# Linear attention and self-attention of a perceiver kernel: scores of a whole token tile issued over four row groups, outcomes of two or four units together, one sum moved to GpSimd

## The reference, cut to what matters

```python
# linear attention: 16 heads of 32; rho is a decay per token and head
S = r * S + (1.0 - r) * jnp.einsum('bhv,bhk->bhvk', v_t, k_t)
y_t = jnp.einsum('bhv,bhvk->bhk', q_t, S)
# self-attention: 16 heads of 64, rotary q and k, causal
scores = jnp.einsum('bhqd,bhkd->bhqk', q, k) * scale
attn = jax.nn.softmax(jnp.where(causal, scores, -jnp.inf), axis=-1)
ctx = jnp.einsum('bhqk,bhkd->bhqd', attn, v)
```

## Time and profile before

| | us |
|---|---|
| median of 3 runs | 2023.27 (2022.45 to 2024.18) |
| the profiled execution's own time | 2018.79 |
| its span | 2017.1 |
| PE busy | 1900.9 (94%), 10722 matmul instructions |
| PEld busy | 1293.5 (64%) |
| DVE busy | 691.0 (34%) |
| ACT busy | 561.0 (28%) |
| POOL busy | 201.3 (10%) |
| mean granted TensorE clock | 0.976 |

### The profile page before, as it was taken

The page is one execution under the profiler, slowest core; times in us unless marked ns, Lnnn a source line. Parts: engine busy times, 40 slices in busy tenths (PEclk is TensorE's granted clock), DMA queues, the critical chain, the costliest instruction groups (busy, mean ns, idle before and its releaser), DMA issues.

```text
span 2017.1 us, 26698 instructions
## 1 busy us (share of the span) xinstructions
PE 1900.9 (94%) x10722; PEld 1293.5 (64%) x10722; DVE 691.0 (34%) x1706; ACT 561.0 (28%) x1263; POOL 201.3 (10%) x293
## 2 busy tenths in 40 slices
PE   5999999999999999998999978999898999999995
PEld 3677777777548447555777755777545544777773
DVE  4234344343335654421000145555425322111111
ACT  2333333332123224212222235444425200111110
POOL 0000000000010232322111031111001110000001
PEclk9999999999999998999999998999899999999998
DMA  5011111101320010027999730102212300877762
GB/s 194 22 42 43 37 69 43 42 22 64 125 104 1 21 42 30 36 83 259 352 354 352 277 119 32 48 32 90 105 42 84 149 22 16 318 289 285 284 252 80
DMA packets 43802, 245.19 MB, mean 122 GB/s; under 512 B 5929, under 2 KB 6433, under 8 KB 20880
## 3 DMA queue, kind: packets, MB, share of 16 engines
q1 hardware_dynamic: 30752, 213.22, 28.7%
q0 software_dynamic: 6000, 17.58, 2.7%
q10 hardware_dynamic: 6912, 12.52, 1.6%
HBM read 227.73 MB, written 15.57 MB: 121 GB/s over the span
## 4 chain that ended last, share of the span: by engine, by line
PE 86%; DVE 5%; issue 5%; DMA 2%; POOL 1%; ACT 1%; POOLq 0%; SPq 0%; DVEq 0%; ACTq 0%
PE bank L224 25%; PE bank L548 25%; PE bank L1606 10%; PE bank L230 8%; PE bank L690 3%; PE bank L718 2%; PE bank L2483 2%; PE bank L637 2%; PE bank L644 2%; PE bank L1186 2%; PE bank L1590 1%; PE bank L983 1%; PE bank L997 1%; PE bank L1211 1%; PE bank L975 1%
## 5 line engine op out<-in xcount | busy, mean ns | idle before, releaser
L548 PE MATMUL bank<-split 128*128 128x512 f32 x2208 | 549.1, 401 | 24.9 <-DVE split L521 12.3
L548 PEld LDWEIGHTS bank<-split 128*128 128x128 f32 x2208 | 407.3, 190 | 155.6 <-issue 31.6
L224 PEld LDWEIGHTS bank<-arena,weights 128*128 128x128 f32 x1984 | 229.7, 187 | 36.1 <-issue 33.7
L224 PE MATMUL bank<-xnT,weights 128*128 128x512 f32 (+1 forms) x592 | 246.7, 577 | 4.7 <-DVE xnT L880 3.1
L224 PE MATMUL bank<-arena,weights 128*128 128x128 f32 (+1 forms) x1984 | 245.1, 282 | 2.8 <-DVE arena L1597 1.8
L224 PEld LDWEIGHTS bank<-xnT,weights 128*128 128x128 f32 x592 | 113.2, 193 | 132.1 <-issue 124.8
L1606 PE MATMUL bank<-weights,arena 128*128 128x512 f32 (+1 forms) x368 | 166.6, 596 | 0.0
L230 PE MATMUL bank<-weights,arena 128*128 128x512 f32 x288 | 131.9, 611 | 8.3 <-ACT arena L2366 6.0
L1606 PEld LDWEIGHTS bank<-weights,arena 128*128 128x128 f32 (+1 forms) x368 | 65.9, 190 | 72.6 <-issue 72.6
L2593 DVE SCALAR_TENSOR_TENSOR arena<-bank,cols,arena 128x128 f32<-128x128 f32 x96 | 28.8, 345 | 230.7 <-PE bank L224 227.9
L230 PEld LDWEIGHTS bank<-weights,arena 128*128 128x128 f32 x288 | 54.8, 196 | 73.3 <-issue 62.9
(11 more groups left out here) (284 smaller groups left out, 2014.5 us busy)
## 6 DMA issues: line engine op xcount, KB each, us to landing
weights<-in_L_ffn_re_w SPq DMA_DIRECT2D x62, 1024.0 KB, 8.2
weights<-in_L_w SPq DMA_DIRECT2D x20, 1408.0 KB, 12.0
arena<-in_ctxT SPq DMA_DIRECT2D x24, 1024.0 KB, 5.0
arena<-in_L_w SPq DMA_DIRECT2D x12, 1408.0 KB, 7.6
weights<-in_L_w_full SPq DMA_DIRECT2D x10, 1280.0 KB, 9.5
expert_out<-arena ACTq DMA_DIRECT2D x47, 256.0 KB, 8.3
weights<-in_L_ffn_sw SPq DMA_DIRECT2D x9, 1024.0 KB, 5.0
arena<-in_L_w_full SPq DMA_DIRECT2D x6, 1280.0 KB, 9.8
```

The costliest lines, as they stand in the source:

```text
L224: s = pe.matmul(out, w[:, k, j0:j0 + m], rhs(k), start=(k == 0), stop=(k == KT - 1))
L548: s = pe.matmul(bank[:, :], still, moving, start=(n == 0), stop=(n == len(order) - 1))
```

## The change

**Linear stage.** TensorE issues the scores of all four units of a token tile together, 16 matmuls of the source into four banks, the strip (row group) changing from one to the next, and the outcomes of the four units of a tile together as 16 matmuls of 32 columns, each into the partitions of its own strip of one bank. They are issued when the spread of the next tile's first unit has been issued. The spreads get two banks, `decay` eight buffers. GpSimd forms mask - L_j for each unit (`less`, four buffers), and VectorE adds it to the spread in one instruction of 512 columns. ScalarE copies the outcome of a whole tile at once (four copies of 128 partitions for sixteen of 32).

**Self-attention stage.** The scores of a tile are likewise issued together over four row groups into four banks, which all have to be read by the mask instructions before those of the next tile may start. Transposes have two banks, outcomes one, values one. The outcomes of two units are issued together as 8 matmuls of 64 columns in two column groups, and one VectorE instruction of 128 partitions adds the bias for both. `self_probT` has four buffers for two. The value groups 3 to 7 move to units 1, 3, 5, 7 and 9.

```diff
     def linear_tensor(pe):
+        def scores(i):
+            if i:
+                pe.wait_ge(lin_decayed.sem, lin_decayed.at(4 * i))
+            for hm in range(KT):
+                for j in range(4):
+                    r = 32 * j
+                    s = pe.matmul(banks[j][:, hm * P:(hm + 1) * P], lin_vT[r:r + 32, hm, i * P:(i + 1) * P],
                                   lin_qT[r:r + 32, hm, i * P:(i + 1) * P], start=True, stop=True)
+            s.then_inc(lin_scored.sem, 1)
+
+        def outcome(i):
+            pe.wait_ge(lin_decayed.sem, lin_decayed.at(4 * i + 4))
+            if i >= 2:
+                pe.wait_ge(lin_out, i - 1)
+            for hm in range(KT):
+                for j in range(4):
+                    r, h = 32 * j, 4 * hm + j
+                    s = pe.matmul(banks[6 + i % 2][r:r + 32, hm * P:(hm + 1) * P], k_tok[:, i, 32 * h:32 * h + 32],
+                                  decay[(4 * i + j) % 8][:, hm, :], start=True, stop=True)
+            s.then_inc(lin_valued.sem, 1)
+
+        for t in range(LN):
+            i, j = LIN_UNITS[t]
+            if t >= 2:
+                pe.wait_ge(lin_logged, t - 1)
+            for hm in range(KT):
+                c = i * HEADS + 4 * hm + j
+                s = pe.matmul(banks[4 + t % 2][:, hm * P:(hm + 1) * P], lg["L"][:, c:c + 1].to_broadcast([P, P]),
+                              ident[:, :], start=True, stop=True)
+            s.then_inc(lin_spread.sem, 1)
+            if j == 0:
+                scores(i)
+                if i:
+                    outcome(i - 1)
+        outcome(NT - 1)
...
     def linear_vector(dve):
-                for hm in range(KT):
-                    c = i * HEADS + 4 * hm + j
-                    s = dve.scalar_tensor_tensor(out=decay[t % 4][:, hm, :], in0=banks[3 + t % 3][:, hm * P:(hm + 1) * P],
-                                                 scalar=lg["minus_L"][:, c:c + 1], in1=mask_ji[:, :], op0=ALU.add,
-                                                 op1=ALU.add)
-                s.then_inc(lin_logged, 1)
+                dve.wait_ge(lin_pool.sem, lin_pool.at(2 + t + 1))
+                if t >= 8:
+                    dve.wait_ge(lin_valued.sem, lin_valued.at((t - 8) // 4 + 1))
+                dve.tensor_tensor(decay[t % 8], blocks(banks[4 + t % 2][:, :], KT), less[t % 4],
+                                  ALU.add).then_inc(lin_logged, 1)
...
     def linear_gpsimd(pool):
+        for t in range(LN):
+            i, j = LIN_UNITS[t]
+            if t >= 4:
+                pool.wait_ge(lin_logged, t - 3)
+            pool.tensor_tensor(less[t % 4], over_middle(mask_ji[:, :], KT), over_last(blocks(lg["minus_L"], NT)[:, i, j::4], P),
+                               ALU.add).then_inc(lin_pool.sem, 1)
...
-    VALUES_FIRST, VALUES_THEN, VALUES_AT = (0, 1), (2,), {0: 3, 1: 4, 4: 5, 8: 6, 12: 7}
+    VALUES_FIRST, VALUES_THEN, VALUES_AT = (0, 1), (2,), {1: 3, 3: 4, 5: 5, 7: 6, 9: 7}
...
     def selfattn_tensor(pe):
+        def scores(i):
+            if i == 0:
+                pe.wait_ge(rope_v, 8 * 2)
+            else:
+                pe.wait_ge(self_masked.sem, self_masked.at(4 * i))
+            for hm in range(KT):
+                for half, (qq, kk) in enumerate(((q1, k1), (q2, k2))):
+                    for j in range(4):
+                        r = 32 * j
+                        s = pe.matmul(banks[j][:, hm * P:(hm + 1) * P], qq[r:r + 32, hm, i * P:(i + 1) * P],
+                                      kk[r:r + 32, hm, i * P:(i + 1) * P], start=(half == 0), stop=(half == 1))
+            s.then_inc(self_scored.sem, 1)
+
+        def outcome(pair):
+            if pair >= 1:
+                pe.wait_ge(self_out.sem, self_out.at(pair))
+            pe.wait_ge(self_prob.sem, self_prob.at(2 * pair + 2))
+            for hm in range(KT):
+                for half in range(2):
+                    h, m = 4 * hm + 2 * (pair % 2) + half, 2 * pair + half
+                    s = pe.matmul(banks[6][64 * half:64 * half + 64, hm * P:(hm + 1) * P], v_tok[:, i, 64 * h:64 * h + 64],
+                                  self_probT[m % 4][:, hm, :], start=True, stop=True)
+            s.then_inc(self_valued.sem, 1)
+
         for t in range(LN + 3):
+            if t < LN and t % 4 == 0:
+                scores(t // 4)
             if t in VALUES_AT:
                 values(VALUES_AT[t])
             if 2 <= t < LN + 2:
+                turn(t - 2)
+            if t >= 4 and t % 2 == 0:
+                outcome(t // 2 - 2)
```

More of the change, by code:

```diff
@@ L927, in build_program @@
     decay = [L(KT, P) for _ in range(4)]
+    L(3 * SEQ)
+    decay += [L(KT, P) for _ in range(4)]
+    less = [L(KT, P) for _ in range(4)]
     G = NT * HEADS
@@ L1001, in linear_tensor @@
+        outcome(NT - 1)
+        pe.wait_ge(lin_out, NT)
         output_tensor(pe, 1, yT, ["lin_o"], xn)
@@ L1079, in linear_scalar, with outcome @@
             act.copy(lin_vT[:, m, :], banks[m][:, :]).then_inc(lin_a.sem, 1)
-        for t in range(LN + 2):
-            if t < LN:
-                act.wait_ge(lin_logged, t + 1)
-                act.activation(decay[t % 4], decay[t % 4], ACT.Exp).then_inc(lin_exped.sem, 1)
-            if t >= 2:
-                n = t - 2
-                i, j = LIN_UNITS[n]
-                r = 32 * j
-                act.wait_ge(lin_valued.sem, lin_valued.at(n + 1))
-                act.copy(yT[r:r + 32, :, i * P:(i + 1) * P], blocks(banks[6 + n % 2][r:r + 32, :], KT)).then_inc(lin_out, 1)
+        def outcome(i):
+            act.wait_ge(lin_valued.sem, lin_valued.at(i + 1))
+            act.copy(yT[:, :, i * P:(i + 1) * P], blocks(banks[6 + i % 2][:, :], KT)).then_inc(lin_out, 1)
+        for t in range(LN):
+            act.wait_ge(lin_logged, t + 1)
+            act.activation(decay[t % 8], decay[t % 8], ACT.Exp).then_inc(lin_exped.sem, 1)
+            if t % 4 == 1 and t > 4:
+                outcome(t // 4 - 1)
+        outcome(NT - 1)
         def roots(i):
@@ L1117, in build_program @@
     soft = [L(KT, P) for _ in range(4)]
-    self_probT = [L(KT, P) for _ in range(2)]
+    self_probT = [L(KT, P) for _ in range(4)]
     pos, turns = L(SEQ), L(SEQ)
@@ new lines, in turn @@
+        def turn(m):
+            if m >= 2:
+                pe.wait_ge(self_prob.sem, self_prob.at(m - 1))
+            pe.wait_ge(self_normed, m + 1)
+            for hm in range(KT):
+                s = pe.transpose(banks[4 + m % 2][:, hm * P:(hm + 1) * P], soft[m % 4][:, hm, :], ident[:, :])
+            s.then_inc(self_turned.sem, 1)
+        def outcome(pair):
+            i = pair // 2
+            if pair % 2 == 0:
+                pe.wait_ge(self_a.sem, self_a.at(4 * KT + 2 * (i + 1)))
+            if pair >= 1:
+                pe.wait_ge(self_out.sem, self_out.at(pair))
+            pe.wait_ge(self_prob.sem, self_prob.at(2 * pair + 2))
+            for hm in range(KT):
+                for half in range(2):
[3 more added lines that the diff above has]
+            s.then_inc(self_valued.sem, 1)
```

128 lines of the change are left out of this document (31 added, 97 removed).

## The result

The changed kernel takes 1990.5 us (median of 4 runs, 1988.3 to 1996.9) where the kernel before, measured beside it, takes 2022.9 (4 runs, 2019.1 to 2024.2). The ratio is 0.9847, with a 95% interval of 0.9829 to 0.9864: faster by 32 us. The forecast was 1998.3: the direction held, the gain was larger than forecast, and the time lies inside the range. Most of the mechanism held as well; the price of the clock in the second stage did not.

What follows compares the result with a forecast made beforehand. TensorE was taken to end both stages, 135.5 us together. Winning 3 us in the linear and 22 in the self-attention stage, 25 off the median 2023.3, gave 1998.3 us; 80% range 1986 to 2012.

Steps and rivals of the forecast that it cites:

- Overlap of row and column groups: Scores and outcomes, both stages: four row or column groups of matmuls run at once, 0.111 us per four.
- no overlap: Rival, chance 0.05: row groups serial, scores cost 3.6 us per linear and 7.1 per self tile; 2030 us.
- The linear cycle: Linear stage, per unit: the VectorE and ScalarE chain of sum, exp and product sets the cycle, 2.16 us.
- the rival of exclusion: Rival, chance 0.05: GpSimd and VectorE exclude each other in the linear stage, 1.04 us more per unit; 2011 us.
- The tile boundary: Linear stage: VectorE waits for the spread behind scores and outcome on TensorE, 0.95 us at each of three boundaries.
- The clock in the linear stage: Half clock at one boundary, the last outcome and the projection takes 7 of 9.7 us won; 3 stay.
- The self-attention stage at full clock: Self-attention stage: TensorE-paced part 32.4 us, then ScalarE exps, last scores and tail; sum 55 us, 30 won.
- The clock in the self-attention stage: Half clock near the start, late in the self-attention stage and in its projection takes 8 us; 22 stay.
- Clock holds: Rival, chance 0.14: full clock in both stages, 40 us won less 4 or so for the tails; 1987 us.
- Half clock throughout: Rival, chance 0.04: half clock through both stages, self-attention 87 us, linear 50 to 52; 2032 us.
- only two row groups: Rival, chance 0.12: only two row groups overlap, score time doubles, 3.6 us more in linear, 7 in self-attention; 2008 us.
- Nothing behind takes it back: Rest of the program: expert stretches are TensorE-bound and weights are requested by use, so later stages lose nothing.

Runs made afterwards that it cites:

- strip-by-strip order: Changed kernel with all score matmuls of one row group issued before those of the next, in both stages: 2035.9 us, ratio 1.0067 to the kernel before.
- the kernel with fillers throughout: Changed kernel plus unread 512-column matmuls before the linear stage's last outcome and, from the third unit, each spread except the second strip's: 1986.5 us, ratio 0.9819.
- the two kernels with fillers: Changed kernel plus unread matmuls ahead of the linear stage's last outcome only (1992.7 us), or also ahead of most spreads (1986.5 us).
- the runs with this stage alone: Changed kernel with the self-attention stage put back as in the kernel before, only the linear stage changed: 2019.0 us, ratio 0.9984.
- all of them together: Changed kernel plus filler matmuls (at spreads, first and last strip only), old tile's outcome behind the new tile's second spread, value groups at 1, 5, 9, 13, 15: 1977.9 us.
- the outcome later: Changed kernel with the old tile's linear outcome issued behind the new tile's second spread instead of ahead of it: 1990.6 us, ratio 0.9830.
- the values later: Changed kernel with value groups 3 to 7 at units 1, 5, 9, 13, 15 in place of 1, 3, 5, 7, 9: 1989.6 us, ratio 0.9827.

## Why the prediction was right or wrong

**Overlap of row and column groups: right.** This carried the forecast. The forecast was 0.9 us for 32 linear score matmuls and 1.8 for 64 self ones; measured, with a change of shape in each, 1.11 and 2.00. Two row groups, or none, would have given twice or more. The estimate that was drawn from the Trainium skill (TensorE: Matmul & The Clock Gate, "Measured speedup vs the span model", 3.07 times for four row tiles) would have made the linear group 32 x 0.111 / 3.07 + 0.20 = 1.36; the trace has 1.11, so here it was close to four times. The strip-by-strip order comes near the rival "no overlap", which was to decide below some 1.3 times: 2.75 us per group, which is 1.4 times (0.111 for 0.080), and a time above that of before. The forecast had priced that rival at 2030. The order came to 2035.9, but not by the rival's sum: of its 45 us over the changed kernel some 20 are the order at full clock, the rest goes with half clock.

**The linear cycle: right in kind, 0.17 us too long.** Sum starts at 607.05 and 609.03, in the lines

```profile
607.05 0.68 DVE L1061 TENSOR_TENSOR arena<-bank,arena 128x512 f32<-128x512 f32 x1
608.42 0.69 DVE L1054 TENSOR_TENSOR arena<-bank,arena 128x512 f32<-128x512 f32 x1 [0.70 <-ACT arena L1091]
609.03 0.68 DVE L1061 TENSOR_TENSOR arena<-bank,arena 128x512 f32<-128x512 f32 x1
```

give 1.98 for the 2.16 of the sum. The sum follows 0.61 us after the start of the product ahead of it (609.03 - 608.42), before that product's 0.69 has ended, and the forecast had laid them end to end. `less` takes 1049 ns for the 1.04 forecast, VectorE's sum beside it 684 ns for 0.69, and GpSimd waits for VectorE, not the other way: the rival of exclusion is out.

**The tile boundary: mis-sized.** The forecast gave 0.95 us to each of three, at full clock. With the clock held, in the kernel with fillers throughout, sums on either side of a boundary stand 614.81 - 611.37 = 3.44 apart, 1.45 more than a cycle (L1066 is the sum there, L1002 the spread):

```profile
611.37 0.68 DVE L1066 TENSOR_TENSOR arena<-bank,arena 128x512 f32<-128x512 f32 x1
...
614.81 0.69 DVE L1066 TENSOR_TENSOR arena<-bank,arena 128x512 f32<-128x512 f32 x1 [1.31 <-PE bank L1002]
```

The path was right: scores, outcome and the new tile's second spread follow each other on TensorE. Its length was not. VectorE has the spread 3.36 us after the end of the old tile's last product (611.45), where the forecast had 3.12: the spread's group takes 1.16 us until its result is there, not 0.89. And VectorE wants it 1.9 us after that product, not 2.16, as its cycle is shorter. In the changed kernel the three are 5.01, 4.96 and 6.14 apart, 10.1 us in excess of three cycles. The longer cycle (15 x 0.17 = 2.6 us) and the shorter boundary (3 x 0.5 = 1.5 us) of the forecast largely cancelled: its full-clock stage was 40.3, and the stage with a clock of 1.00, fillers included, takes 40.2. That they meet so closely is luck.

**The clock in the linear stage: right as a total.** 7 of 9.7 us were to go to half clock, 4.3 at the end and 2.7 at one boundary. Measured by the two kernels with fillers, 45.5 - 40.2 = 5.2 in the stage and 11.55 - 8.77 = 2.8 in the projection: 8.0. There were four falls (611.8, 622.0, 632.3 and 645.9) and not two, so boundaries paid more and the end less than forecast; the second profile of the changed kernel has three. What stays is 4.6 - 2.8 = 1.8 us for the 3 of the forecast, and the runs with this stage alone agree (ratio 0.9984).

**The self-attention stage at full clock: right as a sum.** 55 us were forecast. Taking from 58.0 what half clock cost, 1.5 at the first scores (3.47 for 2.00) and 1.4 at 789.34 (0.5 for the transposes, 0.9 for the outcome), leaves 55.1. Its two parts were right as well. The first, with three scores, five value groups, seven transposes and three outcomes, ends where the last value group does, at 771.78: 34.0 us after the start, less 1.5 of half clock, is 32.5 for the 32.4 forecast; in the second profile, without half clock, it takes 32.6. What follows takes 24.0, less 1.4, which is 22.6 for 22.5.

**The clock in the self-attention stage: the step that failed.** 8 us of the 30 were to go; 2.9 went. At the start it cost 1.5 us for the 1.7 forecast, but only in this execution: in the second profile the first scores run at full clock. The end was not as forecast in either: of 1.8 for the last scores, 2.2 for outcomes and transposes and 2.5 for the projection, only 1.4 came. The last scores, at 775.83, still ran at full clock (2.07), the fall came only at 789.3 and was over at 792.7, and the projection ran at 1.00 throughout. The forecast took half clock as given there because TensorE has 7 us of work in 20. In the trace the clock stood at 1.00 through waits of 0.8, 0.8 and 2.1 us, and fell at the end of the one of 3.0. In the second profile it fell at the end of the same wait of 2.1 us too, which makes 2.3 us at the end; there as well the last scores (2.07) and the projection ran at full clock. What decides between the two for one and the same wait stays open.

**What made the number high.** In executions the gain was 30.0 for the 25 forecast. The terms: +2.7 in the self-attention stage, +2.5 in its projection, -1.2 in the linear stage and its projection, -0.6 from the start of the stage, +1.4 in the rest of the program (4.8 of the 5.0, the rest is rounding). The remaining 2.8 us of 7.8 come from the offset: the forecast put the median 4.5 above its execution, and it lies 1.7 above it (1990.54 for 1988.84).

**The rivals.** "Clock holds" (1987) is nearer in number than the forecast, but not its mechanism: the clock fell, four times in the linear stage, where it had held at 1.00 before. The rule of the Trainium skill that was put beside it (TensorE: Matmul & The Clock Gate, "HAM oscillation") ties the fall to idle gaps of TensorE between bursts. The trace agrees in part: the falls of the changed kernel within the stages lie in or just behind waits of 2.0, 2.2, 4.2 and 3.0 us, and the kernel with fillers has no fall in its linear stage, where the waits are 0.9. But a wait does not decide it: the one of 2.1 us had a fall in one execution and none in the other. And the trace disagrees where TensorE hardly waited. In the kernel before, TensorE was busy all of 752 to 756 and waited only 0.3 and 0.4 us before the fall at 757.6; in the strip-by-strip order it was busy without a gap for 11.9 us and the grant stayed at 0.50. "Half clock throughout" and "exclusion of GpSimd and VectorE" are out, and so is "only two row groups" (whose own terms, 3.6 and 7 us on 1998.3, give 2009, not 2008): the groups took 1.11 and 2.00 us, not 2.0 and 3.8. "Nothing behind takes it back" held: the rest of the program took 1177.9 for 1179.3.

**What stays open.** The rest of the program, the same instructions in all kernels, takes between 1177.9 and 1185.2 us over these executions. These 7.3 us are more than what three of the single edits won in their stages, and so their whole times do not tell them from the changed kernel, though their stages do. Where the stages alone are meant, they are shown; that each of these edits is worth its microseconds in the whole time was only shown for all of them together. The sum of half clock in the rest doesn't order it: 71.4 us of it in the changed kernel (1177.9), 75.2 in its second run (1178.3), 68.3 with fillers throughout (1181.4), 82.1 with the outcome later (1185.2), 88.9 with the values later (1181.9). The traces do show where the difference arises. Over three long stretches, 637 us together (in the changed kernel 923.9 to 1126, 1209 to 1407 and 1729 to 1965), all twelve executions agree within 0.05 us in each. It arises between them, at the stages with waits, and there mostly in step with half clock. The stretch from 1508 to 1638 takes 129.8 to 129.9 us with 10.2 us of half clock, 132.3 with 13.7 and 132.8 to 133.1 with 17.1. Of the 7.3 us of the later outcome over the changed kernel, 2.5 arise at 860 to 924 (13.7 us of half clock for 10.2), 4.0 at 1126 to 1209 (10.2 for 3.4) and 2.4 at 1508 to 1638, less 1.7 at 1407 to 1508 (17.1 for 20.5). Why the clock falls at one of these places in one execution and not in the next stays open; no run was made to settle whether an edit further up decides it.

## What to carry to other kernels

Here small matmuls on different row groups overlapped nearly fourfold only where neighbours in the queue changed group (and bank), so write the loop over the groups innermost, and count a whole tile of them as one burst. For column groups the order was not varied. When a TensorE-bound stage is thinned out, price its gain at both clocks, ahead of and behind every wait, and look at the dense work that follows it; moving needed dense work into the waits (the value groups, 3.4 us of the stage) is worth trying first, since it adds no work, filler matmuls (5.2 us of theirs) after it. Take a second profile of the same kernel before you explain where the clock fell. Read the gain of a small edit from its own stage, and ask of the whole time only what it can tell from its spread.

## What the runs showed of the hardware

- The order of the same matmuls, strips in turn or strip by strip, changed a group of 32 from 1.11 to 2.75 us and the program by 45 us.
- 30 additional matmuls with unread results raised the grant of a stage from 0.84 to 1.00 and shortened it by 5.2 us (4.2 against the changed kernel's second profile).
- After the same wait of 2.14 us the same transposes ran at full clock in one execution of a kernel (0.63 us) and at half clock in another (1.09 us).
- VectorE starts an instruction 0.61 us after the start of one that lasts 0.69.
- TensorE at half clock stayed there for 11.9 us of 32-row matmuls without a gap (strip-by-strip order, 748.56).
